# A graph network's edge stage: the adjacency key product with 12 destinations by 10 classes, both weight parts in one product, GpSimd adding them

## The reference, cut to what matters

```python
h = relu(layernorm(x))
m = mish(mish(concat(h[src], h[dst], edge_attr) @ W1 + b1) @ W2 + b2)   # 40000 x 512
agg = segment_sum(m, dst)
u = mish(concat(h, agg) @ W3 + b3)
x = x + layernorm(h + u @ W4 + b4) * gamma + beta
h = relu(layernorm(x))
s = (h @ U * s) @ Vt
x = x + relu(segment_sum(s[src] * edge_weight[:, None], dst) + bias)
```

## Time and profile before

| | |
|---|---|
| median of 3 runs | 1516.39 us (1514.3 to 1517.26) |
| profiled execution | span 1514.7 us, granted TensorE clock 0.997; the runs' median is 1.7 us more than this span |
| TensorE (PE) busy | 1490.6 us, 98% |
| VectorE (DVE) busy | 1413.2 us, 93% |
| ScalarE (ACT) busy | 1303.0 us, 86% |
| GpSimd (POOL) busy | 1077.3 us, 71% |

### The profile page before, as it was taken

How to read it: one execution, slowest core, us unless ns; L and a number is a source line. 1 busy time by engine, 2 the same in 40 slices (tenths; PEclk the granted TensorE clock), 3 DMA queues, 4 the chain that set the end, 5 groups by cost and what they waited for, 6 DMA issues and landing times.

```text
span 1514.7 us, 33348 instructions
## 1 busy us (share of the span) xinstructions
PE 1490.6 (98%) x7862; PEld 1166.5 (77%) x7862; DVE 1413.2 (93%) x2920; ACT 1303.0 (86%) x2510; POOL 1077.3 (71%) x978
## 2 busy tenths in 40 slices
PE   7989999999999999999999999999999999999998
PEld 6766777777777777777777777777777777777885
DVE  7889999999999999999999999999999999996676
ACT  5088999999999999999999999999999999996562
POOL 1266888788788888878888887888878788863320
PEclk9999999999999999999999999999999999999999
DMA  8866555455555555555555555554555555554773
GB/s 292 271 218 171 120 124 119 114 127 123 119 118 125 118 117 127 122 119 118 125 118 117 124 124 120 118 125 118 116 125 124 120 118 125 118 128 100 175 167 148
DMA packets 124757, 205.10 MB, mean 135 GB/s; under 512 B 31642, under 2 KB 57370, under 8 KB 124721
## 3 DMA queue, kind: packets, MB, share of 16 engines
q0 software_dynamic: 58528, 112.91, 35.1%
q1 hardware_dynamic: 65840, 91.24, 19.5%
q10 hardware_dynamic: 352, 0.52, 0.1%
HBM read 151.60 MB, written 42.75 MB: 128 GB/s over the span
## 4 chain that ended last, share of the span: by engine, by line
PE 94%; DVE 3%; ACT 1%; DMA 1%; issue 1%; SPq 0%; POOL 0%; POOLq 0%; DVEq 0%; ACTq 0%
PE bm L1158 56%; PE bp L1137 7%; PE bp L1145 6%; PE bs L1181 5%; PE bp L1147 5%; PE pm L1169 2%; PE pu L336 2%; PE po L2146 2%; PE pu L2124 2%; PE pB L723 2%; PE pA L723 2%; PE pm L1168 2%; PE pu L2191 1%; DMA M_tab<-zero 1%; PE pu L2178 1%
## 5 line engine op out<-in xcount | busy, mean ns | idle before, releaser
L1062 POOL TENSOR_TENSOR hTl<-tp,hTh 128x512 fp32r<-128x512 f32 (+1 forms) x314 | 414.3, 1319 | 153.6 <-DVE khl L1357 152.8
L1158 PE MATMUL bm<-W2h,hTh 128*128 128x512 f32 x1252 | 499.4, 399 | 1.1 <-DVE bm L1350 0.5
L1158 PE MATMUL bm<-W2l,hTh 128*128 128x512 f32 x1252 | 497.1, 397 | 0.0
L1158 PE MATMUL bm<-W2h,hTl 128*128 128x512 f32 x1252 | 494.6, 395 | 0.0
L1049 POOL DMA_INDIRECT xg<-A_tab,idx x305 | 324.0, 1062 | 102.8 <-issue 79.7
L1158 PEld LDWEIGHTS bm<-W2h,hTh 128*128 128x128 f32 x1252 | 235.7, 188 | 73.3 <-DVE bm L1350 18.7
L1158 PEld LDWEIGHTS bm<-W2l,hTh 128*128 128x128 f32 x1252 | 235.5, 188 | 57.3
L1158 PEld LDWEIGHTS bm<-W2h,hTl 128*128 128x128 f32 x1252 | 235.6, 188 | 53.6
L1217 ACT ACTIVATE rp<-bp 128x512 f32<-128x512 f32 (+1 forms) x314 | 183.8, 586 | 100.4 <-PE bp L1147 98.9
L1321 DVE SCALAR_TENSOR_TENSOR rp<-rp 128x512 f32<-128x512 f32 (+1 forms) x314 | 214.8, 684 | 29.5 <-issue 13.4
L1331 DVE SCALAR_TENSOR_TENSOR tp<-rp,bp 128x512 f32<-128x512 f32 (+1 forms) x314 | 211.8, 675 | 7.6 <-POOL hTl L1062 2.8
(11 more groups left out here) (248 smaller groups left out, 2308.9 us busy)
## 6 DMA issues: line engine op xcount, KB each, us to landing
ea<-in_eaT SPq DMA_DIRECT2D x156, 128.0 KB
M_tab<-mev POOLq DMA_DIRECT2D x157, 80.0 KB, 6.3
agg_tab<-ev POOLq DMA_DIRECT2D x157, 64.0 KB, 2.5
db<-in_dst_rows SPq DMA_DIRECT2D x78, 128.0 KB
M<-M SPq DMA_DIRECT2D x76, 128.0 KB
M_tab<-zero SPq DMA_DIRECT2D x10, 640.0 KB
xg<-A_tab,idx POOLq DMA_INDIRECT x313
eaW<-Bh_tab SPq DMA_DIRECT2D x77, 64.0 KB
```

The costliest lines, as they stand in the source:

```text
L1062: e.tensor_tensor(hTl[p][:, j, 0:w], pick(u, start_t, tp)[:, 0:w], hTh[p][:, j, 0:w], ALU.subtract)\
L1158: last = e.matmul(bank[0:r, :], a[p][:, c, j * P:j * P + r], w[:, c, :], start=False, stop=c == KC - 1 and w is W2l, skip_group_check=True)
```

## The change

The keys become 12 destinations by 10 classes (120 rows, `EC` = 128 columns). The weight goes from the key to the place: VectorE now makes `key`, the plain one-hot of the key (120 elements), and `so` with both weight parts (2 x 128 elements). TensorE makes one product a subtile, of 256 columns, and `pm` then holds for each half group the high parts' sum and the low parts' sum side by side. ScalarE copies 512 columns to a new tile `mw`; GpSimd adds the two sums into `mev`, in an operation of its own in slot 1 (`SUM_LAG`), and its DMAs wait for that. The rows of `M_tab` become 128 elements; its layout per node is the same.

```diff
-EQ = 8
+EQ = 10
 EC = NP // EQ
-EWIN = 16
+EWIN = 12
...
+    SUM_LAG = 5
...
+            def weights(u):
+
+                n = 1 if tail(u) else 2
+                e.wait_ge(a_adj, u.group(1, 1))
+                wait(e, q_adj, u.group(32, -32))
+                e.tensor_tensor(mev[u.par][:, 0:n, :], mw[:, 0:n, 0, :], mw[:, 0:n, 1, :], ALU.add)\
+                 .then_inc(g_mev, 1)
...
                 if half == 0:
-                    e.wait_ge(a_adj, u.group(1, 1))
+                    e.wait_ge(g_mev, u.group(1, 1))
...
+                g = s + -SUM_LAG
+                if g.j == 0 and g.has(MSGS):
+                    weights(g)
...
-                e.matmul(half, khl[i][0:r, 0, :], so[i][0:r, :], start=u.j % HSUB == 0, stop=False, skip_group_check=True)
-                e.matmul(half, khl[i][0:r, 1, :], so[i][0:r, :], start=False, stop=u.j % HSUB == HSUB - 1 or tail(u),
-                         skip_group_check=True).then_inc(s_adj, 1)
+                e.matmul(pm[0:KEYS, h * 2 * EC:(h + 1) * 2 * EC], key[i][0:r, :], so[i][0:r, :, :], start=u.j % HSUB == 0,
+                         stop=u.j % HSUB == HSUB - 1 or tail(u), skip_group_check=True).then_inc(s_adj, 1)
...
-                wait(e, q_adj, u.group(32, -32))
-                n = EC if tail(u) else 2 * EC
-                e.activation(mev[u.par][:, 0:n], pm[:, 0:n], ACT.Copy).then_inc(a_adj, 1)
+                wait(e, g_mev, u.group())
+                n = 1 if tail(u) else 2
+                e.activation(mw[:, 0:n, :, :],
+                             pm[0:KEYS, 0:n * 2 * EC].rearrange("p (h a n) -> p h a n", a=2, n=EC), ACT.Copy)\
+                 .then_inc(a_adj, 1)
...
-                e.tensor_scalar(so[i][0:r, :], iota_q[0:r, :], scol8[0:r, c], None, ALU.is_equal).then_inc(v_adj, 1)
-                e.scalar_tensor_tensor(khl[i][0:r, :, :],
-                                       iota_k[0:r, :].rearrange("p (a k) -> p a k", a=1).to_broadcast([r, 2, KEYS]),
-                                       kcol[0:r, c],
+                e.tensor_scalar(key[i][0:r, :], iota_k[0:r, :], kcol[0:r, c], None, ALU.is_equal).then_inc(v_adj, 1)
+                e.scalar_tensor_tensor(so[i][0:r, :, :],
+                                       iota_q[0:r, :].rearrange("p (a n) -> p a n", a=1).to_broadcast([r, 2, EC]),
+                                       scol8[0:r, c],
                                        wcol_hl[0:r, c, :].rearrange("p a (h k) -> p (a h) k", k=1).bitcast(F32)
-                                       .to_broadcast([r, 2, KEYS]), ALU.is_equal, ALU.mult).then_inc(v_adj, 1)
+                                       .to_broadcast([r, 2, EC]), ALU.is_equal, ALU.mult).then_inc(v_adj, 1)
```

More of the change, by code:

```diff
@@ L274, in gnn_two_layers @@
         ev = [sb(f"ev{i}", [2 * WIN, H]) for i in range(2)]
-        mev = [sb(f"mev{i}", [KEYS, 2 * EC]) for i in range(2)]
+        mev = [sb(f"mev{i}", [KEYS, 2, EC]) for i in range(2)]
+        sb("n_room", [P, 2 * H + HALFN - 2 * H - 4 * EC])
         st, sb_early, _ = scope()
@@ L409, in gnn_two_layers @@
             tb = [sb1(f"tb{i}", [P, H]) for i in range(TB)]
-            sb1("room", [P, 80])
+            sb1("room", [P, 112])
             tbh = [sb1(f"tbh{i}", [P, H], F32R) for i in range(TB)]
@@ L886, in edge_narrow @@
         oh = [sb(f"oh{i}", [P, SUB, WIN]) for i in range(2)]
-        so = [sb(f"so{i}", [P, EC], F32R) for i in range(2)]
-        khl = [sb(f"khl{i}", [P, 2, KEYS], F32R) for i in range(2)]
+        so = [sb(f"so{i}", [P, 2, EC], F32R) for i in range(2)]
+        key = [sb(f"key{i}", [P, KEYS], F32R) for i in range(2)]
+        mw = sb("mw", [KEYS, 2, 2, EC])
         bp = [ps(f"bp{i}") for i in range(2)]
@@ L917, in edge_narrow @@
         a_adj = sem("a_adj")
+        g_mev = sem("g_mev")
         q_adj = sem("e_adjq")
@@ L1086, in adjacency @@
                     e.sem_inc(s_go, 1)
-                e.dma_start(M_d[bass.ds(b * EQ, KEYS), :], mev[u.par][:, half * EC:(half + 1) * EC], accum_op=ALU.add)\
+                e.dma_start(M_d[bass.ds(b * EQ, KEYS), :], mev[u.par][:, half, :], accum_op=ALU.add)\
                  .then_inc(landed, 16)
@@ L1162, in adjacency @@
             def adjacency(u):
-                i, r, half = u.const % 2, ETAIL if tail(u) else P, pm[:, u.j // HSUB * EC:(u.j // HSUB + 1) * EC]
+                i, h, r = u.const % 2, u.j // HSUB, ETAIL if tail(u) else P
                 if u.j == 0:
```

## The result

The changed kernel takes 1576.49 us (median of 4 runs, 1575.97 to 1577.13), before 1516.58: ratio 1.0396, 95% interval 1.0384 to 1.0409. The forecast was 1528 us, its range 1500 to 1546.

A forecast was written before the change was run, and what follows sets the result against it. TensorE bounds now, VectorE 2 to 3% behind; the sum's hold makes VectorE the bound, 16.72 us a group, about 12 us more in 75 groups. 1514.7 + 12 = 1526.7, with 1.7 for the median 1528 us; range 1500 to 1546.

The forecast's parts named there:

- What bounds the kernel: Edge stage: TensorE bounds it, busy 100.00 of 100 us, with VectorE 2 to 3% behind.
- tied in slot 1: At slot 1's message, VectorE's path to the bias copy is as long as TensorE's work, withholding slots 3 and 0's saving.
- TensorE's saving: Key products: 0.10 us a slot, 0.4 a group or 30 us if unheld; 0.20 a group, 15 us, after the tie.
- rival A: GpSimd's sum doesn't hold VectorE, so TensorE's 0.20 us a group counts: 1501 us; chance 0.25.
- Where the sum meets VectorE: Slot 2: GpSimd's sum, behind slot 1's agg_tab DMA, runs beside VectorE's M2 product, comparison and key product, all reading SBUF.
- The size of the hold: Slot 2: the sum holds VectorE 0.90 us a group, between a low end of 0.65 and a high end of 1.31.
- What VectorE can make up: VectorE's waits in a group: 0.47 us behind tp and an estimated 0.2 of smaller ones.
- VectorE's other operations: The plain key comparison, 160 to 120 elements, saves 0.02 us each, 0.08 a group; the product with the weight keeps its form.
- Rival D: Slot 2: the hold comes at its high end, 1.31 us, giving 17.13 a group, +42 us, 1558 us; chance 0.08.
- Rival B: Slot 2: the hold is as short as the sum, 0.74 us; group 16.56 us, time stays at 1516; chance 0.17.
- ScalarE at nothing: Slot 0: the 512-element table copy adds 0.16 us a group, hidden in the 0.90 us wait; uncovered it costs 12 us.
- the kinds of operation that lose: VectorE operations reading SBUF in two streams or a fast mode are held by GpSimd's sum through the shared ports.

## Why the prediction was wrong

- **What bounds the kernel.** Right: TensorE, with VectorE close behind and tied in slot 1. In the kernel without the sum, taking 0.26 us from VectorE gave 0.18 a group back.
- **TensorE's saving.** Right: 0.10 us a slot predicted, 0.10 measured on the mean. The "0.20 a group, 15 us" of rival A, 1501 us, was a little low: the version with the moved sum has 0.23 a group, 1498.9 us, and the one without any 0.27, 1495.0.
- **Where the sum meets VectorE.** Right: in slot 2, on M2 in 54 of 58 groups, beside no PSUM operation.
- **The size of the hold: the step that failed.** "I take 0.90 [...] nearer to the low one because this M2 product has run longer when it is met". The sum took 1.25 us a group, nearly all from M2. The shown 0.39 us of running counted for nothing: M2 ended 0.55 us, nearly a whole operation, after the sum's end, and the next operation started 0.48 us after it. Rows 9 had shown exactly that (0.56 and 0.48), as the upper bound 1.31, and it should have been the value taken: it was the one row with the same VectorE operation, the same kind of DMA ahead and the same order of starts. The 0.35 us missed are 26 us of the 48 by which 1528 fell short.
- **What VectorE can make up.** Mis-sized: 0.47 + 0.20 us of waits predicted, 0.59 recovered (`tp` and `tm`); 6 us.
- **VectorE's other operations.** The key gave 0.04 us net, not 0.08 (3 us); where nothing holds it, in the kernel without the sum, it gave 0.09, so its size was right. That the casts would grow, by 0.23 us a group, 17 us, wasn't in the sum at all; 0.10 of it is there without the sum too. The one-hot gave 0.03 us. The terms make 15.82 + 1.25 + 0.08 + 0.04 + 0.23 - 0.03 = 17.39 us against a mean of 17.39.
- **Rival D**, 1558 us, was the case that came and had 0.08. It too lacked the last two points. Rival B's rule, that whoever starts first keeps the ports, would have given 1516. The Trainium skill (SBUF — State Buffer, SBUF: two separate sides) states it. M2's row at 1001.97 doesn't agree by the shown starts. Of the square's at 1015.99 the first addition's part agrees; of the second, shown starting at 1016.18, the square was 0.19 us ahead and was held through it too.
- **ScalarE at nothing** was right to within 4 us: its longest wait for TensorE is 1.2 us, and the kernel with the moved sum, which has the same copy of 512 columns, still gains.

The prediction named the kinds of operation that lose: two streams from SBUF, or a fast form. The runs bear this out one by one: M2, square, cast and key lose, `ev` and `tp` don't, and a memset takes nothing from M2. The Trainium skill says so (SBUF — State Buffer, Who interferes with whom): with at most one source in SBUF and outside the two-port modes VectorE doesn't contend, with two it contends only against a GpSimd operation that reads. The rows shown here agree: `ev` and `tp` keep 0.69 us beside additions, M2 0.68 beside the memset. What the prediction didn't do is look for the place where none of these stands, 3 us further up in GpSimd's own order.

Open stays what sets the size of the hold behind a DMA's issue: why an operation shown 0.39 us ahead of the addition is held to its end with 256 columns and let through with 128, and why one addition takes more than its own length. GpSimd's shown starts behind a DMA's issue overlap that issue, so the true order may differ from the shown one. Two things speak for that. The square at 1012.92 would have been over at 1013.60, ahead of the sum's shown start at 1013.65, and still lost 0.64 us. And with the addition in the kernel before, M2 shown 0.50 us or more ahead was never held, at 0.44 and less always. Neither tells when GpSimd truly begins to read.

## What to carry to other kernels

Before GpSimd gets an operation that reads SBUF, list for each place in its order what VectorE does there; beside operations with a source in PSUM the addition costs next to nothing (4 us of 1500), beside square, cast or two-source operations in SBUF, and behind a DMA's issue, up to 1.4 us each time. When the trace holds one collision of the kind in question, even in the run-in, take its number and not a value between the bounds. And where two engines are within 3% of each other, a saving on one is worth only what the other leaves, here 21 us of an estimated 30.

## What was not expected of the hardware

- An addition of 120x256 held a VectorE operation in SBUF to 0.55 us after its shown end, whether that one is shown starting 0.39 us ahead of it (M2) or 0.51 us behind the start of the two (the square). Two additions back to back held the square through both, 1.57 us; two of 128 columns each, behind a DMA's issue, let M2 through after 0.93.
- The cast of M2 takes 0.51 us in the changed kernel; its mean before is 0.44. In both it lies beside a GpSimd DMA's issue, so the issue alone isn't the cause: it starts 0.4 us behind the issue's start now, and started 0.6 behind it before. The DMA and the cast in the changed kernel:

```profile
1007.12 1.01 POOL L1099 DMA_DIRECT2D M_tab<-mev  x1
```

```profile
1007.53 0.51 DVE L1313 CAST M<-ea 128x512 fp32r<-128x512 f32 x1
```

- Two accumulating products of 128 columns pass in 0.17 us (start to the transposes' start), one of 256 in 0.12, two of 160 in 0.18.
